# GpSimd issues the gathers of the second layer's last block three steps ahead of their use; two until then

## The reference, cut to what matters

```python
def _L1_ffn_ref(x, up, down, perm):
    b, l, Dm = x.shape                     # 32, 128, 2048
    h, d = (up.shape[0], up.shape[1])      # 16 heads of 128
    unperm = jnp.argsort(perm)
    t = x.reshape(b * l, Dm)
    t = t[:, perm]
    t = t.reshape(b * l, h, d)
    t = jnp.einsum('bhd,hdm->bhm', t, up)      # 128 -> 512
    t = jax.nn.gelu(t, approximate=False)
    t = jnp.einsum('bhm,hmd->bhd', t, down)    # 512 -> 128
    t = t.reshape(b * l, h * d)
    t = t[:, unperm]
    return t.reshape(b, l, Dm)
x = x + _L1_ffn_ref(_L1_cond_ref(x, ...), ...)
```

## Time and profile before

| | us |
|---|---|
| median of 3 executions | 2666.89 |
| lowest and highest of them | 2665.24, 2671.48 |
| the profiled execution's own time | 2668.66 |
| its span, from the first to the last instruction | 2666.7 |
| PE busy in the span | 2576.5 |
| ACT busy in the span | 1003.1 |
| POOL busy in the span | 957.7 |

### The profile page before, as it was taken

How to read it: one execution, slowest core, us unless ns; L and a number is a source line. 1 busy time by engine, 2 the same in 40 slices (tenths; PEclk the granted TensorE clock), 3 DMA queues, 4 the chain that set the end, 5 groups by cost and what they waited for, 6 DMA issues and landing times. The chain is left out here.

```text
span 2666.7 us, 39124 instructions
## 1 busy us (share of the span) xinstructions
PE 2576.5 (97%) x12090; PEld 2112.6 (79%) x12090; DVE 1835.0 (69%) x2671; ACT 1003.1 (38%) x1631; POOL 957.7 (36%) x835
## 2 busy tenths in 40 slices
PE   8899999999999999999999999999999999999885
PEld 6678888888888788887888778888888888888674
DVE  6555555865555755475444768888888888888675
ACT  3211112311122322232222555555555555555562
POOL 2275645456554454233223212222222222222221
PEclk9999999999999999999999999999999999999997
DMA  9855644765545667475545744667767777677667
GB/s 307 303 182 181 203 162 150 253 196 199 187 161 182 224 219 221 155 252 192 164 155 182 222 143 131 181 218 219 216 215 220 219 218 219 217 217 218 191 195 229
DMA packets 419587, 541.04 MB, mean 203 GB/s; under 512 B 36440, under 2 KB 273840, under 8 KB 419376
## 3 DMA queue, kind: packets, MB, share of 16 engines
q1 hardware_dynamic: 317168, 305.04, 38.3%
q10 hardware_dynamic: 77376, 154.27, 15.4%
q0 software_dynamic: 24832, 79.16, 9.2%
HBM read 309.72 MB, written 228.61 MB: 202 GB/s over the span
## 5 line engine op out<-in xcount | busy, mean ns | idle before, releaser
L427 PE MATMUL ps_c<-w_hi,ring_hi 128*128 128x512 f32 x1792 | 714.3, 399 | 12.7 <-DVE r_early L931 6.7
L427 PE MATMUL ps_c<-w_hi,ring_lo 128*128 128x512 f32 x1792 | 708.5, 395 | 0.0
L427 PE MATMUL ps_c<-w_lo,ring_hi 128*128 128x512 f32 x1792 | 708.3, 395 | 0.0
L574 ACT ACTIVATE ring_hi<-raw_n 128x512 fp32r<-128x512 f32 x384 | 240.7, 631 | 896.2 <-DVE raw_n L871 243.9
L1295 POOL DMA_INDIRECT y_d<-y_s,idx x128 | 147.5, 1152 | 750.5 <-ACT y_s L1465 644.3
L427 PEld LDWEIGHTS ps_c<-w_hi,ring_hi 128*128 128x128 f32 x1792 | 338.4, 189 | 92.2 <-DVE ring_lo L910 13.4
L1432 ACT ACTIVATE kern<-ps_up 128x512 f32<-128x512 f32 x512 | 306.5, 599 | 261.2 <-PE ps_up L1318 242.6
L427 PEld LDWEIGHTS ps_c<-w_hi,ring_lo 128*128 128x128 f32 x1792 | 338.0, 189 | 79.8
L427 PEld LDWEIGHTS ps_c<-w_lo,ring_hi 128*128 128x128 f32 x1792 | 338.4, 189 | 76.7
L1550 DVE TENSOR_TENSOR g_lo<-kern,g_hi 128x512 fp32r<-128x512 f32 x512 | 354.7, 693 | 48.5 <-ACT g_hi L1436 32.1
L931 DVE TENSOR_TENSOR r_early<-ps_c,r_early 128x512 f32<-128x512 f32 x256 | 176.8, 690 | 286.3 <-PE ps_c L427 286.2
(11 more groups left out here) (199 smaller groups left out, 3852.8 us busy)
## 6 DMA issues: line engine op xcount, KB each, us to landing
u_d<-raw_n ACTq DMA_DIRECT2D x64, 512.0 KB, 3.2
x_d<-r_early ACTq DMA_DIRECT2D x128, 256.0 KB, 3.4
x_d<-x_s ACTq DMA_DIRECT2D x128, 256.0 KB, 2.7
raw_n<-u_d SPq DMA_DIRECT2D x64, 512.0 KB, 3.5
u_s<-x_d SPq DMA_DIRECT2D x496, 64.0 KB, 2.7
z_d<-x_s SPq DMA_DIRECT2D x120, 256.0 KB
rear<-y_d SPq DMA_DIRECT2D x120, 256.0 KB, 6.2
rear<-x_d SPq DMA_DIRECT2D x112, 256.0 KB
```

Of the source, the lines that this page charges most:

```text
L427: mm = nc.tensor.matmul(bank, a[:, dc, :], w[k][:, dc, :], start=(first and dc == 0 and n == 0), stop=(dc == 3 and n == 2), skip_group_che ...
L574: nc.scalar.activation(ring_hi[g % RING][:].rearrange("p a n -> p (a n)"), ring_raw[p][k], ACT.Copy).then_inc(hi_ready, 1)
```

## The change

In the last block POOL issues a gather at position x for step x+3 where it issued the one for step x+2. To make the transition, position 111 issues two gathers, for steps 113 and 114. The buffers, the wait on `tlo_ready` in `gather` and all work of the other engines stay.

```diff
+        def ahead(k, h):
+
+            return isinstance(k, int) and H * k + h >= STEPS - H
+
@@
-                if exists(k, h, 2):
+                if exists(k, h, 2) and not ahead(k, h):
                     if isinstance(k, int) and H * k + h == -2:
                         pool.wait_ge(small_in, 32)
                         pool.wait_ge(xlo_ready, H - 1)
...
                         gather(k, h + 2, parity)
                     else:
                         gather(k + 1, h + 2 - H, 1 - parity)
+                if isinstance(k, int) and H * k + h == STEPS - H - 1:
+                    gather(k + 1, 2, 1 - parity)
+                if ahead(k, h) and exists(k, h, 3):
+                    gather(k, h + 3, parity)
                 if exists(k, h, 0):
                     s, j = H * k + h, h % 2
                     pool.wait_ge(y_ready, s + 1)
```

## The result

The changed kernel takes 2652.18 us (median of 7 executions, 2649.39 to 2658.57), the kernel before 2665.58 us beside it (median of 7, 2664.42 to 2671.48). The ratio is 0.995, with a 95% interval of 0.994 to 0.996: 13.4 us less. The profiled execution took 2651.15 us, with a span of 2649.3.

The account below looks back on a forecast made before the run. In the last block, a loop through the late gather was taken to bound each step. Gains of 3.6 + 11.6 = 15.2 us took the profiled 2668.66 to 2653.5, as a median 2651.7, said as 2652; range 2648.5 to 2658.

Parts of the forecast that it names:

- What bounds a step: Last block: scatter, gather, split and y_s form a loop with one gather landing in each step, 7.16 us a step.
- The step of 6.19 us: Last block, gather already there: ACT's order sets 4.45 + 0.49 + 0.52 + 0.73 = 6.19 us; PE alone needs 5.99.
- The 12 steps, 11.6 us: Steps 113 to 125: 6.19 instead of 7.16 us each, 11.6 us less, including some 1.7 us of slow clock.
- The first gain, 3.58 us: Step 115's gather goes out earlier, so y_s of step 113 comes at 2523.14 instead of 2526.72, 3.58 us earlier.
- a rival for all steps: Last block: a late load (rear<-y_d) holds PE's turn ahead of the down product; part of a rival case given 0.14.
- Position 111's two gathers: nothing: At the transition, issuing step 114's gather right behind step 113's is hidden and costs nothing; if not hidden, 1.3 us.
- the signs of being wrong: PE or DVE waiting for rear, a gap ahead of POOL's gather, or step 113's gather landing later than 3.3 us.
- the 3.2 of the bound: Position 111: if its two gathers shared the engines evenly, step 113's would come 3.2 us later at most.
- Each gather in time: Last block: gathers land before ACT's split, some 5 us to spare; the tightest, step 116's, has 2.6 us left.
- The end: nothing: Behind the last step, scatter, loads, turns and stores move as a whole; the change costs 0 there.
- Another loop: Rival for the last block: steps settle at 6.68 us, gain 9.4 us, 2657.5; chance 0.14 together with both bounds.
- the slower case: Rival: SP's load landings back up to 16 us, the step takes 8.25 us, 2676.4 us in all; chance 0.04.

Follow-up runs that it names:

- e6: Kernel before the change, with five small memsets on POOL ahead of each gather from step 114 on: 2699.57 us, ratio 1.0127.
- e7: Changed kernel, with five small memsets on POOL ahead of each gather from step 114 on: 2653.03 us, ratio 0.995 to the kernel before.
- e2: Kernel before the change, with y_s ahead of the split on ACT from step 110 on: 2653.15 us, ratio 0.995.
- e11: Changed kernel, with gathers three ahead from position 109 and the split sooner on both ACT and DVE: 2637.91 us, ratio 0.9893 to the kernel before.
- e3: Changed kernel, with y_s ahead of the split on ACT as well: 2653.69 us, ratio 0.995 to the kernel before.
- e8: Changed kernel, with gathers three ahead from position 109 and the split sooner on ACT only: 2647.98 us, ratio 0.9932 to the kernel before.
- e10: Changed kernel measured again, nothing altered: 2651.71 us, ratio 0.9941 to the kernel before.
- e4: Changed kernel, with gathers three steps ahead from position 109 instead of 112 (108 issues two): 2642.57 us, ratio 0.9912 to the kernel before.
- e9: Repeat of the changed kernel with gathers three steps ahead from position 109: 2644.12 us, ratio 0.9911 to the kernel before.
- e12: Another repeat of the changed kernel with gathers three steps ahead from position 109: 2644.01 us, ratio 0.9919 to the kernel before.

## Why the prediction came out right, by its own steps

- **What bounds a step.** Right, and shown from two sides. A delay of 1.6 us ahead of each gather costs 33 us in the kernel before and nothing in the changed one (e6, e7), and taking y_s out from behind the split gives the change's gain without touching a gather (e2).
- **The step of 6.19 us, set by ACT's order.** The size was right: 6.21 measured. That ACT sets it is shown by the down product that starts 0.15 us behind y_s, and by e11: once the split left the place between the third gelu and y_s and DVE's half moved with it, that gap went and the step fell to 5.98, against the 5.99 read for PE alone. e3 and e8 show another side of the order, which the prediction didn't need: where the split reaches PE later (behind y_s in e3, behind the delayed g_lo in e8), the up products wait instead.
- **The 12 steps, 11.6 us.** Right: 85.91 - 74.54 = 11.37 us. The text goes too far only where it puts one landing in each step. The gather of step 116 was not waited for in the kernel before; its step took 7.74 us by the slow clock behind the stall, which the prediction counts as some 1.7 us in this term.
- **The first gain, 3.58 us.** From y_s of step 110 (2499.55 before, 2496.86 after) to that of 113 it took 27.17 us before and 24.98 after: 2.2 us, and 3.5 in e10 (2499.37 to 2523.05). The term is right in e10 and 1.4 short in the first profile. I had costed everything ahead of the split of step 115 at nothing; but how the slow stretch behind step 111's stall falls is not the same in each execution. And in e7, where step 112 was quick (7.56), PE then waited 1.75 us at its turn of step 113 for rear<-y_d, whose load had to wait for the scatter of step 111; in e10, with step 112 at 7.74, the load landed in time. So part of this term can be lost to either. The late load was in the prediction only as a rival for all steps, and it came in just one.
- **Position 111's two gathers: nothing.** Right. The gather of step 113 landed 2506.09 - 2502.66 = 3.4 us behind its issue, where it had been 3.31. By the letter this is one of the signs of being wrong (later than 3.3 us), but 0.1 us is nothing beside the 3.2 of the bound.
- **Each gather in time.** Right: from step 115 on no split waited. The gather of step 116, issued at 2518.37, landed 6.1 us later, at 2524.5, by the view of its tile, and was used at 2527.56; 3.1 us were left where the prediction had 2.6. The eleven gathers behind it took 3.4 to 4.6 us. The Trainium skill's rule of the queues that take turns (in "DMA: Bandwidth & Descriptors", section "Queues, rings and completion order"), by which the landing stays at 6.48, agrees with this. It isn't proven by it: a load of SP, issued at 2516.74, landed at 2524.5 as well, 7.8 us behind its issue, and a gather that had to queue behind that load could have landed at the same time.
- **The end: nothing.** From y_s of step 127 to the end of the span it was 44.3 us before (2622.40 to 2666.7), and 43.1 after. Three executions of one kernel (e4, e9, e12) give 44.7, 43.0 and 42.8, so these 1.2 us can't be put down to the change.
- **The rivals.** Another loop did not hold the steps: 232 GB/s and no wait of PE for rear. (The 5 tiles a step that the prediction gives to SP are SP's three and POOL's gather and scatter; its figure in GB/s holds all five.) The landing of SP's loads had a median of 4.2 us instead of 5.4, so the slower case was far off.

The sum was 15.2 us, and the medians say 13.4 (first set) and 15.6 (e10 against its own kernel before, 2667.30). That the forecast of 2652 and the measured 2652.18 fall together so closely is luck: the sum was taken from a kernel before of 2666.9 us, which beside the changed kernel took 1.3 less, and the gain was 1.8 smaller. In the first pair of profiles the span shrank by 17.4 us, of which 2.7 lie ahead of y_s of step 110, where the two kernels have the same program; that is scatter between executions, and its cause stays open.

## What to carry to other kernels

When a transfer lands a little late in each step, read which instruction of the waiting engine stands behind the wait, and who needs that one: here it was not the split data that PE lacked, but a copy queued behind the split. Issuing the load one step earlier and moving the copy ahead of the wait both removed it, and were worth the same; together they were worth no more. Once the load is early, the place of the waiting work among its neighbours is the next bound, and it has to be moved on all engines that share it, or the gain turns into a loss.

## What the runs showed of the hardware that wasn't expected

- Behind a stall of PE of 3.5 us, the number of matmuls at the lower of the two clocks differs between executions of the same kernel: the step behind it took 9.02 us in one and 7.74 us in another. Without the stall it takes 6.2 (e4), so the slow stretch cost 1.5 to 2.8 us on top of the stall itself.
- A delay on the chain was paid 1.6 times over: five small memsets that put 1.6 us ahead of the gather made the step 2.5 us longer (e6), as the gather itself also landed later, after 4.83 us on average instead of 3.79. Why it did stays open.
